# Layer 1's feed-forward stage: who splits its weights, and when GpSimd starts on the low parts of y

## The reference

```python
x_in = x
h = film(rmsnorm(x, norm2_w), cond, film2_w, film2_b)
h = jax.nn.gelu(h @ mlp_w1 + mlp_b1, approximate=False) @ mlp_w2 + mlp_b2
return x_in + h
```

## Time and profile before

| | us |
|---|---|
| median of three executions | 2101.91 (2098.63 to 2109.48) |
| the profiled execution | 2115.73 |
| its span, first to last instruction | 2114.0 |
| VectorE busy in the span | 1483.4 |
| ScalarE busy | 1188.8 |
| GpSimd busy | 805.5 |

### The profile page before, as it was taken

One profiled execution on the slowest core, in us unless ns is written; L12 is line 12 of the kernel. 1 busy time (PEld: TensorE's weight loads), 2 busy tenths in 40 slices (PEclk: granted clock), 3 DMA queues, 4 the chain that ended last, 5 costly groups with the idle time before them and its releaser, 6 DMA issues. The chain is left out here.

```text
span 2114.0 us, 37287 instructions
## 1 busy us (share of the span) xinstructions
PE 1873.8 (89%) x14338; PEld 1192.7 (56%) x14338; DVE 1483.4 (70%) x2500; ACT 1188.8 (56%) x2038; POOL 805.5 (38%) x724
## 2 busy tenths in 40 slices
PE   6988999788989999996888889999999999993786
PEld 3766577677533333333666655555555555492686
DVE  5665743564479897984688777777777777546796
ACT  3332332332228686884556677777777777632463
POOL 3465620174040302001245645554444444304376
PEclk8999999899959897998899989999999999996798
DMA  5000000100533211212256954454445555225453
GB/s 148 0 4 17 3 18 0 61 1 1 154 96 93 49 39 37 55 32 67 90 185 213 298 140 101 112 121 113 101 108 131 127 125 141 61 80 160 140 150 51
DMA packets 196833, 191.40 MB, mean 91 GB/s; under 512 B 64240, under 2 KB 155248, under 8 KB 196400
## 3 DMA queue, kind: packets, MB, share of 16 engines
q1 hardware_dynamic: 193584, 184.82, 32.4%
q0 software_dynamic: 3072, 4.20, 1.1%
HBM read 121.33 MB, written 67.37 MB: 89 GB/s over the span
## 5 line engine op out<-in xcount | busy, mean ns | idle before, releaser
L1568 POOL TENSOR_SCALAR l3h_prob<-l3h_prob,l3h_inv 128x1024 f32<-128x1024 f32 x256 | 288.2, 1126 | 320.8 <-DVE l3h_inv L1540 320.8
L1534 DVE TENSOR_REDUCE l3h_nmax<-l3h_score 128x1 f32<-128x1024 f32 x256 | 313.5, 1225 | 138.0 <-PE l3h_score L1477 137.9
L1758 DVE TENSOR_REDUCE l2h_nm<-l2h_rowb 128x1 f32<-128x1024 f32 x256 | 302.7, 1218 | 43.0 <-PE l2h_rowb L1689 42.7
L1793 ACT ACTIVATE l2h_pT<-l2h_score 128x512 f32<-128x512 f32 x512 | 274.7, 597 | 97.0 <-PE l2h_score L1711 74.5
L1558 ACT ACTIVATE l3h_prob<-l3h_score,l3h_nmax 128x1024 f32<-128x1024 f32 x256 | 285.8, 1117 | 38.5 <-DVE l3h_nmax L1534 3.6
L1500 PE MATMUL l3h_out<-l3h_pT,l3h_vs 128*64 128x512 f32 x1024 | 274.4, 617 | 0.0
L1526 ACT ACTIVATE l3h_pT<-l3h_ring 128x512 f32<-128x512 f32 x256 | 152.8, 597 | 104.4 <-PE l3h_ring L1488 103.9
L1488 PEld LDWEIGHTS l3h_ring<-ident,l3h_prob 64*128 64x128 f32 x4096 | 173.2, 139 | 35.5 <-issue 8.0
L1524 DVE COPY l3h_pT<-l3h_ring 128x512 f32<-128x512 f32 x256 | 172.1, 672 | 2.0 <-PE l3h_ring L1488 2.0
L1488 PE MATMUL l3h_ring<-ident,l3h_prob 64*128 64x64 f32 x4096 | 169.4, 222 | 2.2 <-DVE l3h_pT L1524 2.0
L1725 PE MATMUL l2h_out<-l2h_pT,l2h_vs 128*32 128x256 f32 (+1 forms) x1792 | 166.1, 445 | 0.0
(11 more groups left out here) (456 smaller groups left out, 4354.4 us busy)
## 6 DMA issues: line engine op xcount, KB each, us to landing
q3first<-l_q SPq DMA_DIRECT2D x64, 256.0 KB, 5.1
l3h_Q<-l_q SPq DMA_DIRECT2D x64, 256.0 KB, 5.0
l_q<-l3qkv_hi SPq DMA_DIRECT2D x16, 512.0 KB, 4.7
l_q<-l3qkv_lo SPq DMA_DIRECT2D x16, 512.0 KB, 3.4
l_k<-l3qkv_hi SPq DMA_DIRECT2D x16, 512.0 KB, 3.0
l_k<-l3qkv_lo SPq DMA_DIRECT2D x16, 512.0 KB, 3.0
k3first<-l_k SPq DMA_DIRECT2D x64, 128.0 KB, 5.1
l3h_vs<-l_v SPq DMA_DIRECT2D x32, 256.0 KB, 3.1
```

What stands on the lines that cost most here:

```text
L1534: dve.tensor_reduce(self.nmax[:, t % 4:t % 4 + 1], self.score[t % 2][:, :], AX.X, ALU.max, negate=True).then_inc(self.maxes, 1)
L1568: pool.tensor_scalar(self.prob[:, q, :], self.prob[:, q, :], self.inv[:, q:q + 1], self.vscale, ALU.mult, ALU.mult).then_inc(self.scaled, 1)
L1758: dve.tensor_reduce(self.nm[:, mr % 2, at:at + 1], self.rowb[h][:, :], AX.X, ALU.max, negate=True).then_inc(self.maxes, 1)
L1793: act.activation(self.pT[:, g % 4, h, c * C:(c + 1) * C], self.score[v % 3][:, :], ACT.Exp).then_inc(self.exps, 1)
```

## The change

ScalarE makes the high parts of quarters 2 to 7 in one go, directly behind the scaling of chunk 0 and ahead of the square root of chunk 3, and none behind Gelus. VectorE makes the low parts of all eight quarters: those of 0 and 1 where it did, then it splits chunk 0, then takes the statistics of chunk 3 (the two have changed places), then makes the low parts of 2 to 7, and only then the high parts of y. GpSimd makes no low parts of weights; it also doesn't wait for the high part of chunk 0 of x any more, and makes the four bias additions of a chunk behind the eight low parts of y of this chunk instead of ahead of them. TensorE's and SyncE's programs are unchanged.

```diff
         @block.gpsimd
         def _(pool):
-            pool.wait_ge(xhs, KF)
-            for q, (src, hi, lo) in enumerate(quarters):
-                if q < 2:
-                    continue
-                pool.wait_ge(whs, q + 1)
-                pool.tensor_tensor(lo, src, hi.bitcast(F32), ALU.subtract).then_inc(wls, 1)
             pool.wait_ge(loaded, 32)
             for c in range(NC):
-                for t in range(c * TC, (c + 1) * TC):
-                    pool.tensor_tensor(xb[:, t, :], X[:, t, :], b2[:, :], ALU.add).then_inc(xbs, 1)
                 if c >= 2:
                     pool.wait_ge(downs, (c - 1) * 2)
                 for j in range(F):
...
                     pool.tensor_tensor(yp[1][:, c % 2, j, :], y[:, n % 4, :], yp[0][:, c % 2, j, :].bitcast(F32),
                                        ALU.subtract).then_inc(yls, 1)
+                for t in range(c * TC, (c + 1) * TC):
+                    pool.tensor_tensor(xb[:, t, :], X[:, t, :], b2[:, :], ALU.add).then_inc(xbs, 1)
...
             high(range(2))
             nt.act_scale(act, 0)
+            high(range(2, 8))
             nt.act_root(act, 3)
-            high(range(2, 4))
             act.wait_ge(loaded, 32)
...
-                    if n in (3, 4):
-                        high((2 * n - 2, 2 * n - 1))
...
+            def low(quads, made):
+                for q in quads:
+                    src, hi, lo = quarters[q]
+                    dve.wait_ge(whs, q + 1)
+                    dve.tensor_tensor(lo, src, hi.bitcast(F32), ALU.subtract).then_inc(made, 1)
+
             nt.dve_norm(dve, 1)
-            for q in range(2):
-                src, hi, lo = quarters[q]
-                dve.wait_ge(whs, q + 1)
-                dve.tensor_tensor(lo, src, hi.bitcast(F32), ALU.subtract).then_inc(first_lo, 1)
+            low(range(2), first_lo)
+            split(0)
             nt.dve_stats(dve, 3)
-            split(0)
+            low(range(2, 8), wls)
```

## The result

Over 20 executions of each kernel, the changed kernel's median is 2101.88 us and that of the kernel before 2109.81, a difference of 7.9 us. The measured ratio, which is not that of the two medians, is 0.9956, 95% interval 0.9938 to 0.9974: 9.3 us of 2110, with anything from 5.5 to 13.1 us inside the interval. The forecast gain, 9 us or 0.43%, agrees with this. The forecast time, 2093, is 9 us too low, and 2101.88 lies outside the range of 2086 to 2100. The forecast was subtracted from a median of three executions, 2101.91, which lay 8 us under the median of all 20. Three executions lie far out (6694 us of the changed kernel, 2250 us of the kernel before and 4256 us of the version with the block cut, both in the last set); they are counted in the medians and left out of the ratios.

What follows compares the result with a forecast made beforehand. TensorE, busy 89% of the span, was taken to be held in this stage by an 11.0 us hole traced to GpSimd's queue. The turn at 423.1 instead of 432.29 gives 9 us: 2101.9 - 9 = 2093 us, range 2086 to 2100.

Steps and rivals of the forecast that it cites:

- The hole and its chain: TensorE's 11.0 us wait before the turn of chunk 2, traced through GpSimd's queue; turn at 423.1 instead of 432.29.
- y_hi 1 is caught, to 414.7: VectorE's second high part of y waits behind GpSimd's y_lo 0, which runs from 413.2 to 414.5.
- rival B: Shorter chain to the turn: VectorE ahead of GpSimd at each meeting, gain 12.4 us, or clock stays high; chance 0.30.
- None of this moves the turn by itself: VectorE splitting chunk 0 before the statistics starts matmuls 2.95 us earlier, but alone leaves the turn of chunk 2 unmoved.
- it costs one for one if w2 lands later: ScalarE's six high parts before the first Gelu cost nothing, unless w2 lands later than 408.5.
- The rest is a shift: From the turn of chunk 2 on, the program runs as now; the 9 us reach the kernel's end.
- B's clock half: Clock stays high over the shorter hole of 4.8 us; turn and some six matmuls 2.2 us shorter, 2090.7.
- C: GpSimd catches every VectorE operation before the turn: turn at 430.2, gain 2.1 us, 2099.8; with late weights, chance 0.13.
- D: Granted clock stays at 0.50 through chunks 0 and 1: 12.3 us lost against 9 gained, 2105.2; chance 0.04.
- E: Low parts of y did not hold the turn; another wait ends there at the same time: 2101.9; chance 0.03.
- B with both halves: VectorE first at each meeting and clock staying high over the hole together; lower end of the range, 2086.
- 2101.9 - 9: Median of the runs shown less the 9 us by which the turn of chunk 2 comes earlier: 2093 us.

Runs made afterwards that it cites:

- the version with the block cut: GpSimd's sixteen bias additions in layer 2's heads cut in four blocks: on the kernel before, 0.9948; on the changed kernel with chunk 2's normalisation early, 0.9884.

## Why the prediction was right in its steps and wrong in its time

*The hole and its chain.* Right: w2's high parts from 408.19 (408.1), table load at 410.50 (410.6), last weight subtraction at 411.35 (411.3), first low part of y at 413.10 (413.2), the turn at 422.97 (423.1). "Two of the four normalisations are caught" is what happened. One meeting went otherwise: "y_hi 1 is caught, to 414.7" took 0.43 us from 413.10, as in the first half of rival B. It moved nothing, since the next high part had to wait for its Gelu until 415.01.

*What hides each part.* Right: "None of this moves the turn by itself" (the swap, 0.1 us), "it costs one for one if w2 lands later" (5.6 for 5.6), the additions behind the low parts. The prediction did not say that the moved additions on GpSimd, worth 2.0 us alone, are worth 0.2 once the weights are gone.

*The rest is a shift.* Nearly: counted from the stage's first turn, the gain is 9.4 us at the turn of chunk 2 and 10.1 at the end of the stage. Of the difference, 0.4 us is a shorter wait in the second product (1.0 against 1.4 us) and 0.3 a shorter stretch on the low clock, 3.5 us from the turn against 4.1: the seventh matmul of chunk 1 starts 3.92 us behind the turn instead of 4.24. Layer 2 starts 10.1 us earlier.

*Rivals.* B's clock half did not hold: the clock was at 1.00 through the hole and at 0.51 from 423 to 424, in the turn. C and D are excluded by the turn at 422.97 and by 0.98 behind it. E named 2101.9, the time that was measured, but that is chance: E has the turn where it was, and it came 9.3 us earlier.

*Slips in the working.* "B with both halves" adds up to 2101.9 - 12.4 - 2.2 = 2087.3, not 2086. The clock rose some 4.4 us behind the first matmul of chunk 0, not "within 4 us" (the windows have 0.50 up to 412 and a mean of 0.74 from 412 to 413). The 0.27 taken from B's 0.30 is nine tenths of it, where the text says two thirds and more. None of these moves the forecast.

*The step that failed* is the level: "2101.9 - 9", with "3 us of measurement". Single executions of the kernel before have a standard deviation of 6 us, so the median of three, 2101.91, was not known to 3 us; over 20 executions it is 2109.81. The profiled execution, 13.8 above it, was the warning: the prediction only asked whether the cut scales with it, when it was evidence on the median. With 2109.8 the same sum gives 2100.8, 1.1 us under the measured time. A large part of the spread has a place: in the eleven traces of kernels with the block whole, the heads took 366 to 376 us in the four where the longest cast was 3.6, and 383 to 388 in the seven where it was 4.8, and cutting the block took away the long cast and 0.52% of the time, 11 us. What decides in one execution which way the cast falls is not known; nor is the cause of the rest of the spread, 3 to 4 us.

## What to carry to other kernels

Follow the hole back through every engine's queue, and count each instruction in it; a move pays only for what stands ahead of the last wait, and moves that shorten the same queue need not add. Before a forecast of an absolute time, take the spread of single executions from all of them, the profiled one too; with three, allow their whole range and more. Look for long blocks of GpSimd's instructions over a short VectorE instruction that TensorE waits for, in stages far from the change as well.

## What the runs showed of the hardware that was not expected

A VectorE cast caught by back-to-back GpSimd instructions got in after one of them (0.70 us) or only after the whole block (4.82 us for 0.17 us of work), in the same program. The Trainium skill, "SBUF — State Buffer", section "Terms", describes a lock that VectorE and GpSimd take for one whole instruction. The 0.70 agrees, and so do the 3.59 us behind one instruction of 3.62; the 4.82, over seven instructions of 0.69, does not follow from that alone.

A hole of 4.6 us in TensorE's work ended with the granted clock still at 1.00, and over the next microsecond, with the engine busy again, it was at 0.51: here the hole was paid for after its end, with 3.5 us of matmuls on the low clock.
